# A Mamba2 block and a ternary FFN on one core: order of three DMAs per tile, of one VectorE operation in the last tile, and of one semaphore increment

## The reference, cut to what matters

```
x = layernorm(x + block(x))        # x: 2 sequences x 2048 tokens x 256
x = layernorm(x + ffn(x))

block(x): h = x + mamba2(rmsnorm(x)) ;  return h + (relu(rmsnorm(h) @ w_fc)**2) @ w_proj
mamba2:   z, xbc, dt = split(xn @ w_in)
          xc = silu(conv4(xbc)) -> xh, B, C ;  dt = softplus(dt + dt_bias)
          per chunk: y = (C B^T * decay) @ (dt xh) + C @ state * decay + d_skip * xh ; state update
          return rmsnorm(y * silu(z)) * norm_w @ w_out
ffn(x):   h = silu(x W1 * s1) * (x W2 * s2) ; h = gelu(h H1 * sh1) ; h = gelu(h H2 * sh2) ; return h W3 * s3
```

## Time and profile before

| | |
|---|---|
| median of three runs | 1231.27 us (1230.64 to 1232.23) |
| profiled execution, its own time | 1230.64 us |
| span of the profile | 1228.8 us |
| PE busy | 1202.0 us, 98% |
| DVE busy | 775.3 us, 63% |
| ACT busy | 646.1 us, 53% |
| POOL busy | 232.8 us, 19% |
| granted TensorE clock | 0.998 of full speed |
| DMA | 68.37 MB, 15.9% of 16 engines' span |

### The profile page before, as it was taken

The page is one execution under the profiler, slowest core; times in us unless marked ns, Lnnn a source line. Parts: engine busy times, 40 slices in busy tenths (PEclk is TensorE's granted clock), DMA queues, the critical chain, the costliest instruction groups (busy, mean ns, idle before and its releaser), DMA issues.

```text
span 1228.8 us, 19228 instructions
## 1 busy us (share of the span) xinstructions
PE 1202.0 (98%) x6524; PEld 1012.8 (82%) x6524; DVE 775.3 (63%) x1356; ACT 646.1 (53%) x1213; POOL 232.8 (19%) x210
## 2 busy tenths in 40 slices
PE   8899999999999999999999999999999999999996
PEld 6678888888888888788888888888888888888885
DVE  6798898989899898855426336254362362543633
ACT  7788888888787888666214123142241331422420
POOL 0527162534434352610000000000000000000000
PEclk9999999999999999999999999999999999999999
DMA  8221221122222221135300001001000010010000
GB/s 292 71 82 74 82 74 62 53 81 75 96 75 96 75 88 49 67 126 228 136 1 10 26 1 34 0 0 34 0 18 16 0 34 0 0 34 0 18 1 18
DMA packets 31128, 68.37 MB, mean 56 GB/s; under 512 B 3952, under 2 KB 22512, under 8 KB 29168
## 3 DMA queue, kind: packets, MB, share of 16 engines
q1 hardware_dynamic: 31088, 67.84, 15.9%
HBM read 59.43 MB, written 22.03 MB: 66 GB/s over the span
## 4 chain that ended last, share of the span: by engine, by line
issue 53%; POOL 0%; DVE 0%; POOLq 0%; DVEq 0%
POOL rsv_b L1864 0%; DVE o_sb L1934 0%; POOLq L1862 0%; DVEq L1706 0%; POOL rsv L235 0%; POOLq L441 0%
## 5 line engine op out<-in xcount | busy, mean ns | idle before, releaser
L1850 ACT ACTIVATE full<-bank,scale 128x512 f32<-128x512 f32 x128 | 88.3, 690 | 383.9 <-PE bank L1756 383.9
L1756 PE MATMUL bank<-hB_lo,h_sb 128*128 128x512 f32 x512 | 200.2, 391 | 0.0
L1756 PE MATMUL bank<-hB_hi,h_sb 128*128 128x512 f32 x512 | 199.6, 390 | 0.0
L1756 PE MATMUL bank<-hA_hi,h_sb 128*128 128x512 f32 x512 | 199.3, 389 | 0.0
L1756 PE MATMUL bank<-hA_lo,h_sb 128*128 128x512 f32 x512 | 199.2, 389 | 0.0
L1910 DVE CAST hA_hi<-full 128x512 fp32r<-128x512 f32 x64 | 27.3, 427 | 185.8 <-ACT full L1850 185.8
L1864 POOL TENSOR_TENSOR rsv_b<-mv_b,eps 128x4 f32<-128x4 f32 x8 | 10.7, 1340 | 624.3 <-DVE mv_b L187 624.3
L1756 PEld LDWEIGHTS bank<-hA_hi,h_sb 128*128 128x128 f32 x512 | 96.1, 188 | 20.1
L1756 PEld LDWEIGHTS bank<-hA_lo,h_sb 128*128 128x128 f32 x512 | 96.1, 188 | 20.1
L1756 PEld LDWEIGHTS bank<-hB_hi,h_sb 128*128 128x128 f32 x512 | 96.2, 188 | 19.2
L1756 PEld LDWEIGHTS bank<-hB_lo,h_sb 128*128 128x128 f32 x512 | 96.2, 188 | 19.1
(11 more groups left out here) (227 smaller groups left out, 2984.8 us busy)
## 6 DMA issues: line engine op xcount, KB each, us to landing
chk_xh<-w_ffn SPq DMA_DIRECT2D x16, 704.0 KB, 4.3
ffn_raw<-w_ffn SPq DMA_DIRECT2D x8, 1408.0 KB, 6.8
h_sb<-ffn_raw SPq DMA_DIRECT2D x2, 4096.0 KB, 19.0
xT<-x_t SPq DMA_DIRECT2D x8, 512.0 KB, 6.0
x_res<-x SPq DMA_DIRECT2D x8, 512.0 KB, 3.8
x_rows<-x SPq DMA_DIRECT2D x8, 512.0 KB, 3.3
x_in<-x_rows SPq DMA_DIRECT2D x8, 512.0 KB, 4.4
x_in<-x SPq DMA_DIRECT2D x7, 512.0 KB, 4.6
```

What stands on the lines that cost most here:

```text
L1756: ins = pe.matmul(o, a_, b_, start=first and n == 0, stop=last and n == 1, skip_group_check=True)
L1850: nc.scalar.activation(full[:, n % FULL, :], b[:], ACT.Gelu, scale=scale[:, 1 + n // KH, n % KH:n % KH + 1]).then_inc(s_gd, 1)
```

## The change

There are three edits. In SP's `tile`, `load_residual(i)` goes ahead of `load_xT(i + 1)` and `spread_rstd(i + 1)`, and the wait for `s_rsl` is gone. In DVE's `iteration`, for the last tile alone, `scores(2)` goes behind `mask_exponents(3)` and `gate(1)`. The semaphore `s_gd` is now declared with those of the second block, and ACT's increment of it is ACT's first step in the second block, behind the barrier.

```diff
@@ SP, tile(i, ...)
+                    load_residual(i, at)
                     if at_xT is not None:
                         load_xT(i + 1, at_xT)
                         spread_rstd(i + 1)
-                        sp.wait_ge(s_rsl, 16 * i + 16)
-                    load_residual(i, at)
                     copy_piece(piece)
@@ ACT, end of the first block
-                act.sem_inc(s_gd, B_ACT_BANKS)
@@ DVE, iteration
                     state(step, i, 1)
-                    if not more:
-                        scores(w, i, 2)
                     mask_exponents(w, 3)
                     gate(w, i, 1)
                     if not mlp:
                         fc_lo(1)
+                    if not more:
+                        scores(w, i, 2)
                     add_out(w, i, 0)
@@ ACT, start of the second block
+                act.sem_inc(s_gd, B_ACT_BANKS)
                 act.wait_ge(s_par, 64)
```

More of the change, by code:

```diff
@@ L315, in post_ln_block @@
         s_s3 = sem("s3_loaded")
-        s_gd = sem("ffn_act_item_drained")
         s_w = [sem(f"{n}_loaded") for n in ("w1", "w2")]
@@ L1694, in post_ln_block @@
         s_gi = sem("ffn_act_item_ready")
+        s_gd = sem("ffn_act_item_drained")
         s_shi = sem("hidden_hi_ready")
```

## The result

The changed kernel took 1238.27 us (median of 4 runs, 1235.75 to 1239.66) against 1231.32 us before (4 runs, 1230.64 to 1232.23). Seven further runs of it lie between 1237.08 and 1243.40. The ratio is 1.0061, 95% interval 1.0043 to 1.0081. Later the same kernel was run again beside others: ratio 1.0056 (1.0042 to 1.0070). So it is 0.6% slower, 7 us. I had forecast no change (1232.1) with a range up to 1237.5: the result is above the range, in the direction of rival A and a little beyond its upper price.

A forecast was written before the change was run, and what follows sets the result against it. The PE bounds the kernel, busy 413.46 of 415 us. On the profiled 1230.64, 0.6 + 0.2 + 0 gives 1231.4; from the median, 1231.27 + 0.8 = 1232.1 us, no change; 8-in-10 range 1229.8 to 1237.5.

The forecast's parts named there:

- rival A: DVE in front of norm_x, six iterations: the spread is late, each loses 0.7 to 1.1 us; 1236.3 us; chance 0.31.
- the term for the spread's delay: Late x_rstd delays norm_x in six iterations and stops the PE: 0.1 us each, 0.6 us in all.
- the row's landing: The 1/rms row, queued behind x_res and xT, lands at 240.5 in tile 3, 1.2 us later; iteration 1, 2.2 later.
- The second leg: The spread after the row's landing, up to x_rstd's landing: takes 4.12 us in tile 3, as before.
- The other way, by the rate of `a_log_b`: Tile 3 at 298 GB/s: row lands at 240.9; costs 0.35 us in five tiles, 0.5 in iteration 1, 2.2 in all.
- the slack: Before norm_x in tile 3: x_rstd landed at 243.40 and was needed at 244.63, so 1.2 us.
- The price of a delay: Each 0.1 us by which norm_x starts late stops the PE 0.1 us, at w_out's weight load, never given back.
- What needs no cover: SP's loads: nothing waits for x_res, so its earlier landing gains nothing; xT is through early enough for norm_x.
- The DVE edit: Last tile: the wait at L650 goes, but y_diag(2) waits for scores(2) and starts at 519.8, +0.2 us, once.
- rival B: Last tile: row isn't held, scores(2) gets ahead of POOL, whole 1.5 us wait gained; 1229.8 us; chance 0.13.
- The increment: Start of second block: ACT's increment stands ahead of its table load, 0.8 us cover it, cost 0.
- Rival C: In the loop: the row lands as late as a_log_b, 19 us, 1250 us; chance 0.06, including anything short of that beyond rival A.

The follow-up runs named there:

- residual_keep_wait: Against the kernel before: residual's load moved ahead of xT and the spread, wait for x_rstd's landing kept in front of the copy of weights; ratio 1.0002.
- copy_behind_only: Against the kernel before: copy of weights issued directly behind the spread, then the wait for x_rstd and the residual's load; ratio 1.0003.
- residual_only: Against the kernel before: only SP's edit, the residual's load ahead of xT and the spread, and no wait for x_rstd; ratio 1.0075.
- all_with_wait: The changed kernel with all three edits, but the wait for x_rstd's landing put back in front of the copy; ratio 1.0017 against the kernel before.
- residual_behind_xT: Against the kernel before: xT left early, residual's load between it and the spread, wait for x_rstd kept in front of the copy; ratio 1.0002.

## Why the prediction was wrong

**The step that failed** is the term for the spread's delay in the sum: "I take 0.1 us per iteration, 0.6 us in all". In it the copy of weights, which "may add to each of these", stood at nothing, and the row's landing was set too early. The runs showed 5.5 us in the loop in one profile and 9.1 in another. Two terms make them up.

- The second leg. I kept it at 4.12 us. In tile 3 of the profile after it is 5.4 up to the start of `norm_x`, 1.3 us more. With the copy held back in the same order (`residual_keep_wait`) its median is 3.8 us, with the copy behind it 4.3 and 5.2 in the two profiles of the changed kernel, and 5.6 with the copy alone (`copy_behind_only`).
- The row's landing. I had 1.2 us later than before. In the profile after it was 1.5 us in tile 3, 1.6 to 2.1 in the other loop tiles, and 2.8 in iteration 1, where I had 2.2. The order of service was right: the row comes right behind `xT`. Nor was the time of the two loads too short. I let their data be through 4.55 us after the issue of `x_res` (240.05 - 235.5). In the windows view of the profile after (length, busy us per engine, PEclk, DMA share, GB/s) the data stop at about 241.75, 4.5 us after 237.26:

```profile
241.50:241.75 0.25, 0.25 (x3) 0.21 (x2) 0.25 (x2) 0.25 (x1) 0.00 (x0) 1.00 1.07 379
241.75:242.00 0.25, 0.25 (x3) 0.21 (x2) 0.25 (x1) 0.25 (x2) 0.00 (x0) 1.00 0.43 72
```

  What was too short in tile 3 is the rest, from the end of these data to the row's landing. I gave it 0.45 us, which no row shows; here it was about 0.7 (242.47 - 241.75). The other way, by the rate of `a_log_b`, gave a row landing at 240.9, 3.0 us after its issue, and was the better one; I took a value nearer to the optimistic end.

The experiments weigh the two. With the row held and the copy kept back, the loop is 1.0 us longer and the ratio is 1.0002, close to the 0.6 us that I had forecast. It is the copy, without a number in my sum, that made a loss of it.

Some readings of mine were off without changing the forecast. The second way for tile 3 ends 0.39 us behind the need (240.9 + 4.12 - 244.63), not within 0.3. The 333 GB/s of the stretch from 245.25 to 246.50 are 416 KB, so `x_res` with its 524 was not quite through at its end. Rival A's 4.2 to 6.6 us are six times 0.7 to 1.1, without the second edit's 0.2.

Why that matters so much is the slack. I read it as 1.2 us and as nearly used up. The experiments agree with that slack: each term alone fits in it nearly whole (loop +1.0 with the held row, +1.5 with the copy), and together they overflow it.

| kernel | row, tile 3 | median landing of x_rstd | loop | time over before |
|---|---|---|---|---|
| before | 1.42 | 4.0 | 401.3 | |
| held row alone (`residual_keep_wait`) | 2.97 | 3.8 | 402.3 | 1.0 |
| copy behind alone (`copy_behind_only`) | 1.40 | 5.6 | 402.8 | 1.3 |
| both (`residual_only`) | 2.94 | 4.8 | 408.5 | 8.3 |
| all edits, two profiles | 2.94, 2.97 | 4.3, 5.2 | 406.8, 410.4 | 7.8 (second) |

The last column compares only runs whose mean granted clock is 0.996 to 0.998, median with median (3 to 22 runs each), so that the clock's part of the noise is out. It goes with the loop; losses of 1 us are within the intervals of the ratios above.

The sum of the two single losses in the loop is 2.5 us, the loss of both 5.5 to 9.1: losses against one slack don't add.

**The price of a delay** was right, its place only half. DVE's 7.4 us, less the 1.6 us by which the six `norm_x` got shorter, are 5.8 and the loop grew by 5.5; in `residual_only` 9.2 less 1.6 are 7.6 against 7.2. I had named the weight load of `w_out` as where the PE stops. Its wait grew only to 5.2 us in six (0.70 each before). The rest is one step earlier, at the second matmul of `exponents(3)`, whose bank DVE's `yT_lo` has to drain, in the waits view of the profile after:

```profile
PEld bank L631 <- DVE yT_lo L1301: 4.1, 5, 1.3
```

**What needs no cover** was right: nothing waits for `x_res`, and its earlier landing gained nothing. `xT` itself, issued 24 us later than before in tile 3 (237.90 against 213.50), still was not late.

**The DVE edit** came out as played: +0.08 us at `y_diag(2)` in all four profiles that have it without the filling, where I had 0.2, and alone no change in time. The gain of rival B did not exist, since POOL's `S` goes between. What I had not forecast is the clock.

**The increment** costs nothing, as forecast, though by less cover than I had read: I took ACT's table load as the sign that its stream was running, and the increment does not come as early before it as I assumed.

**The rivals.** Rival A had the mechanism and the place. I gave it 0.31 and a price of 0.7 to 1.1 us per iteration; the loop lost 0.9 in one profile and 1.5 in the other, for it took the copy's term, which I had not priced. Rival C's mark, a row landing as late as `a_log_b`'s 6.0 us, was not reached by any row. The Trainium skill's rule that I cited for it, that completion can be long when the target is HBM (DMA: Bandwidth & Descriptors, Anatomy of one DMA), would have made the row land well after the load ahead of it. That section describes transfers issued by GpSimd; here SP issues. In the profile after the row landed 0.1 to 0.2 us after `xT` in four iterations, and 0.5 and 0.7 us after it in the iterations 1 and 5, so nothing near the 1.8 us of my estimate showed; what made the two longer is open.

**What stays open.** The clock's fall in the last tile was in two of the four profiles that have the DVE edit without the filling, and in none of the nine without it (the kernel before among them). That is too few to say that it comes of the edit. The kernel before has a stretch there in which the PE is just as idle, 0.51 us busy of 2, and its clock does not fall:

```profile
516.00:518.00 2.00, 0.51 (x4) 0.30 (x3) 2.00 (x3) 0.00 (x0) 2.00 (x3) 1.00 0.00 0
```

Five profiles without the DVE edit have a fall to 0.5 of three to four us elsewhere, between 15 and 42 us. The wait at `y_diag(2)` is 1.45 us in the two with the fall and in the two without it. So the trace shows no difference that decides it. In the last tile the fall goes with 1.1 to 2.1 us more (65.8 and 66.4 against 64.7 and 64.3), of which up to 0.8 us is the PE's wait for the load of x1. For the 1.0017 of `all_with_wait` the fall is not needed: among runs at a mean clock of 0.996 to 0.998 this kernel is 1.4 us over before, as `copy_behind_only` is 1.3. That 5 of its 12 runs have a clock of 0.994 or less, and 7 of 29 of the kernel before, may be the rest; it is argued, not shown.

## What to carry to other kernels

Before a transfer is moved ahead of a small one that something waits for, count what is still in the queue when the small one comes, and count also what will then be issued right behind it; a wait on a landing that looks idle can be what keeps the queue clear (here 1.0002 with it and 1.0075 without it, in the new order). Take the slack at the waiting engine once, and hold the sum of all new delays against it, never each by itself. A term that may add and has no number does not belong in a sum as nothing: when the count ends within 0.4 us of the need and is paid in every iteration, such a term decides the result.

## What the runs showed of the hardware

- A load of 256 KB that reads one row of DRAM for 128 partitions lands in 4.0 us (median of seven), but in 5.6 when a copy of 1408 KB is issued 0.6 us behind it on the same queue. Not every transfer is slowed like that: `x_res` (512 KB of ordinary rows) lands in 3.7 to 4.1 us with the same copy behind it, and in 3.7 to 3.8 in `residual_behind_xT`, where the small transfers of the spread are behind it.
- A store of 2 KB took 1.4 us alone, 1.6 to 2.1 with one 512 KB load issued 2.3 us before it, and 2.9 to 3.6 with two, issued 2.3 and 1.6 us before it. With the two issued 1.4 and 0.9 us before it, in iteration 1, it took 4.2 to 4.8.
- In the last tile, DVE products of two SBUF inputs and POOL's products took turns instruction by instruction: 2.06 us for a DVE one of 1.2, 2.02 for a POOL one of 1.05, and the one that waited came next.
